# A Mamba scan on one core: where the next slot's gate product stands in TensorE's row

## The reference, cut to what matters

```python
xz = xn @ W_in                                  # 512 -> 2 x 1024
xs, res = jnp.split(xz, 2, axis=-1)
xs = silu(causal_conv(xs) + conv_b)
xdbc = xs @ W_xp                                # dt_r (128), B (16), C (16)
delta = softplus(dt_r @ W_dt + b_dt)
h_t = h_{t-1} * exp(delta * A) + delta * B * xs  # for 16 states n of each channel
y = sum_n(h_t * C) + xs * D
y = y * silu(res)                               # the gate
out = y @ W_out + x
```

## Time and profile before

| | |
|---|---|
| median of 3 runs | 1585.88 us (1583.93 to 1586.73) |
| the profiled execution, device time | 1580.36 us |
| its span, first to last instruction | 1578.3 us |
| mean granted TensorE clock | 0.972 of full |
| busy: PE, DVE, ACT, POOL | 1434.1, 1314.4, 744.0, 1077.5 us |
| slots (L1566 of slot 0 to the last sum of slot 31) | 61.7 to 995.9 us |
| shared experts and router after it | about 996 to 1208 us |

### The profile page before, as it was taken

How to read it: one execution, slowest core, us unless ns; L and a number is a source line. 1 busy time by engine, 2 the same in 40 slices (tenths; PEclk the granted TensorE clock), 3 DMA queues, 4 the chain that set the end, 5 groups by cost and what they waited for, 6 DMA issues and landing times.

```text
span 1578.3 us, 14721 instructions
## 1 busy us (share of the span) xinstructions
PE 1434.1 (91%) x4412; PEld 722.2 (46%) x4413; DVE 1314.4 (83%) x1931; ACT 744.0 (47%) x1160; POOL 1077.5 (68%) x545
## 2 busy tenths in 40 slices
PE   6678999899999799999888787999999999999997
PEld 3223444344344344444333333544445666667775
DVE  5589999999999999999999999464656868777772
ACT  4656666767656776655666665342000221211111
POOL 0299998999987999998999989150001446455453
PEclk9889999999999899999999999999999999999999
DMA  4540112510112510102410002231403788888995
GB/s 134 226 179 9 44 31 90 214 42 31 36 32 89 213 42 29 37 22 74 180 35 30 9 20 107 67 114 34 187 32 114 209 229 228 252 234 250 265 245 67
DMA packets 63822, 176.85 MB, mean 112 GB/s; under 512 B 10304, under 2 KB 15168, under 8 KB 55040
## 3 DMA queue, kind: packets, MB, share of 16 engines
q1 hardware_dynamic: 48128, 138.59, 25.4%
q0 software_dynamic: 15616, 37.32, 11.4%
HBM read 142.98 MB, written 32.85 MB: 111 GB/s over the span
## 4 chain that ended last, share of the span: by engine, by line
PE 42%; POOL 25%; DVE 19%; DMA 7%; issue 7%; ACT 1%; POOLq 0%; SPq 0%; DVEq 0%; ACTq 0%
POOL h L1368 14%; DVE h L957 10%; PE bank L1920 8%; PE bank L1569 8%; PE bank L1530 7%; DMA out<-y,slot_token 6%; DVE h L947 4%; POOL h L1355 4%; PE bank L1962 4%; PE bank L1537 4%; PE bank L1466 3%; POOL h L1373 3%; PE bank L1498 2%; PE bank L1488 2%; DVE xs L926 2%
## 5 line engine op out<-in xcount | busy, mean ns | idle before, releaser
L1368 POOL TENSOR_TENSOR h<-h,c_rep 128x2048 f32<-128x2048 f32 x128 | 578.6, 4526 | 20.0 <-DVE h L957 14.8
L1569 PE MATMUL bank<-h,ident 128*128 128x512 f32 x916 | 442.7, 627 | 73.5 <-POOL h L1368 57.8
L728 ACT ACTIVATE bank<-delta,a_neg 128x512 f32<-128x512 f32 x512 | 338.6, 684 | 151.7 <-DVE h L957 150.0
L1569 PEld LDWEIGHTS bank<-h,ident 128*128 128x128 f32 x916 | 181.9, 202 | 312.7 <-issue 219.3
L957 DVE TENSOR_TENSOR_SCAN h<-bank,state,h 128x512 f32<-128x512 f32 x256 | 306.9, 1265 | 1.3
L957 DVE TENSOR_TENSOR_SCAN h<-bank,h 128x512 f32<-128x512 f32 x256 | 291.5, 1204 | 3.7 <-ACT bank L728 2.7
L173 DVE STREAM_TRANSPOSE xT<-xg 32x256 f32<-32x256 f32 (+1 forms) x592 | 247.0, 417 | 24.6 <-DMA xg<-flat,slot_token 16.9
L947 DVE TENSOR_TENSOR h<-bank,b_rep 128x2048 f32<-128x2048 f32 (+1 forms) x105 | 228.8, 2179 | 21.6 <-ACT bank L719 18.3
L1920 PE MATMUL bank<-xT,w_ring 128*128 128x256 f32 x1024 | 227.4, 380 | 0.0
L1920 PEld LDWEIGHTS bank<-xT,w_ring 128*128 128x128 f32 x1024 | 193.8, 190 | 41.2 <-issue 16.6
L1729 POOL DMA_INDIRECT out<-y,slot_token x64 | 101.5, 1586 | 108.4 <-DMA out<-y,slot_token 63.6
(11 more groups left out here) (236 smaller groups left out, 1477.0 us busy)
## 6 DMA issues: line engine op xcount, KB each, us to landing
w_ring<-in_w SPq DMA_DIRECT2D x32, 1024.0 KB
b_rep<-bcd SPq DMA_DIRECT2D x16, 1024.0 KB, 4.8
c_rep<-bcd SPq DMA_DIRECT2D x16, 1024.0 KB, 5.0
w_ring<-in_w SPq DMA_DIRECT2D x32, 512.0 KB
w_in<-in_w_in_x SPq DMA_DIRECT2D x32, 256.0 KB, 2.6
w_res<-in_w_in_res SPq DMA_DIRECT2D x32, 256.0 KB, 2.6
xa<-in_x SPq DMA_DIRECT2D x20, 256.0 KB, 3.1
xb<-in_x SPq DMA_DIRECT2D x16, 256.0 KB, 2.7
```

What stands on the lines that cost most here:

```text
L728: eng.activation(da[j][:], delta[:, g % 2], ACT.Exp, scale=a_neg[:, col:col + 1])\
L1368: ins = eng.tensor_tensor(h[:, q], h[:, q], c_rep[:, Q * q:Q * q + Q, :], ALU.mult)
L1569: ins = eng.matmul(y_ps[:], c.ident[:], h[:, q, j, :], start=False, stop=(q == NQ - 1 and j == Q - 1))
```

## The change

In `gap_items`, z of the next slot goes into gap 1, behind what stands there, instead of gap 2. It stays in gap 2 where the slot g itself is leaving or dense. So 13 of 31 z products move: those made in slots 0, 1, 2, 6, 7, in 14 and 15, in 22 and 23, and in 27, 28, 29 and 30. Besides, in slot 31 the half projection `out` of segment 3 goes from gap 1 to gap 0.

```diff
             if g == LAST - 1:
                 gaps[3].append(("out", NSEG - 1, 0, 0))
             if g == LAST:
-                gaps[1].append(("out", NSEG - 1, 1, 0))
-            gaps[2].append(("z", (g + 1) // DC, g + 1, 0))
+                gaps[0].append(("out", NSEG - 1, 1, 0))
+            gaps[2 if leaving(g) or dense(g) else 1].append(("z", (g + 1) // DC, g + 1, 0))
             gaps[3].insert(0, ("dt", (g + 2) // DC, g + 2, 0))
```

## The result

| | before | after |
|---|---|---|
| median on the same chip | 1585.34 us (1581.91 to 1586.73, 8 runs) | 1577.24 us (1570.03 to 1579.27, 8 runs) |
| ratio | | 0.9939, 95% interval 0.9918 to 0.9960 |
| profiled execution, its span | 1580.36, 1578.3 us | 1579.27, 1577.5 us |
| mean granted TensorE clock | 0.972 | 0.971 |
| first L1566 to the first flat transpose (L1507), "the slots" | 934.2 us | 923.4 us |

The forecast was 1576.9. Two things stand apart from it, though: the slots gained 10.8 us and not 9.0, and in this execution 6.4 of them were lost again in a stretch for which nothing was expected. The eight times of after suggest that this is not always so: three lie at 1570.03 to 1571.54 and five at 1577.13 to 1579.27, with nothing between.

The account below looks back on a forecast made before the run. No engine bounds the whole (chain 42% TensorE, 25% GpSimd, 19% VectorE); GpSimd's 20.2 us of waits can shrink. 4.0 + 3.0 + 2.0 = 9.0 us, from median 1585.88 to 1576.9; gain 5.8 to 11.0, range 1573.0 to 1583.5.

Parts of the forecast that it names:

- Part A: Slots 0 to 2: z moved into TensorE's idle time takes away GpSimd's waits; 4.0 us, at the low clock 1.8.
- The first rival: Slot 2 at the low clock: slots 0 to 2 give only 1.8 us, sum 6.8, 1579.1 us; chance 0.24.
- the working: TensorE's slot 2 timed at full clock: quarter 1 from 139.7, then transposes and z, done at 147.2; GpSimd without wait.
- Part B: Slots 6, 7, 14, 15, 22, 23: z fills idle time ahead of slot 22's quarter 2; 3.0 us, all from slot 22.
- nothing lies in 6, 7, 14, 15 and 23: Moved z in these slots counts nothing: VectorE's busy row hides later sums; behind slot 23 GpSimd spreads nothing.
- Part C: Slots 27 to 31: VectorE's 1.33 us wait goes and the half projection fills idle time; 2.0 us, between 1.5 and 3.9.
- the upper bound of 3.9: Most that slots 27 to 31 could gain; the end at full clock was put at 992.1, against 995.9 now.
- the 1.8 us for a slow opening of slot 31: Price taken for slow d_diag and 16 slow instructions behind about 4 us of TensorE idle time; end 993.9, not 992.1.
- The 1.5 us put on the half projection: Slot 31: lower bound for slots 27 to 31, the moved projection alone, filling 1.48 us of idle time; 1.5 us.
- only slot 31 pays: By the skill's rule each of 13 slots would open slowly; the prediction claimed only slot 31 does.
- Whatever is gained by 996 is passed on whole.: Behind slot 31: TensorE is busy 209.0 of 212 us with shared experts, routed experts follow, so no gain is lost.
- a sign that it is wrong: Prediction is wrong if slots 3 to 7 lose part A's gain or time behind 996 doesn't shift by the same amount.

Follow-up runs that it names:

- the other kernel: The changed kernel with the four int32 casts (L1049) made by GpSimd behind its iotas instead of by VectorE; 1575.89 us median, ratio 0.9919.

## Why the prediction was right, and where it wasn't

**Part A, 4.0 us.** Measured 3.1 in the profiled pair (197.0 to 193.9 us for slots 0 to 5). The first rival, a slow quarter 1 in slot 2, is refuted: 0.16 us idle, 3.70 us, z done at 150.9, where the working gives 147.2 + 3.2 = 150.4 with this execution's later start. GpSimd's half spread at 155.57 waited for nothing. TensorE's stretch ended in slot 3 as worked out, but the sum came 3.4 us sooner and not 4.0, and VectorE still waited 1.77 us (2.10 before) ahead of the convolution at 179.98. Its scans of slot 4 start at 182.47, counted from slot 0's opening 3.1 us sooner, where the forecast had 4.0. One piece was wrong: slot 0's wait shrank from 1.26 to 0.60 us only, since quarter 1 took 6.59 us there behind 6.31 of idle time (5.21 behind 5.95 before), which made the moved z late. And what the sum treated as terms of single slots is one thing that needs all three.

**Part B, 3.0 us.** Measured 3.8 (54.9 to 51.1). The wait of 2.97 us in slot 23 went as forecast. Of the 3.8, 0.5 was only moved: slots 14 to 21 lasted 234.0 instead of 233.5. And part of the 3.8 is the slow sum in slot 22: against executions in which that sum was fast, the part is worth 2.1 us (53.2 to 51.1). That nothing lies in 6, 7, 14, 15 and 23 held.

**Part C, 2.0 us.** Measured 3.8 (126.9 to 123.1), nearly the upper bound of 3.9. VectorE's wait of 1.33 us for delta xs is gone, as forecast. The term mis-sized was the 1.8 us for a slow opening of slot 31 behind about 4 us of idle time. The slow opening came in slot 30 (2.08 us for d_diag, 8.98 for the sixteen instructions), while VectorE was busy without a pause; TensorE's row had no gap behind it, so ahead of slot 31 there were only 1.65 us, and no slow opening. The 1.5 us put on the half projection as the lower bound are right for it alone (1.3), but nothing is left of them beside z, which gives all 3.8.

**The price that the Trainium skill's rule names.** The prediction cited the rule against gathering idle time ("TensorE: Matmul & The Clock Gate", section "HAM oscillation — how this bites in real kernels"). It gathers, and the prediction was wrong that only slot 31 pays. Of the 13 slots that follow a moved z, slots 2, 8, 24, 28, 29 and 30 open more slowly than before (d_diag 1.86 to 2.08 us, 1.12 to 1.46 before, behind 3.02 to 5.40 us of idle time), 7, 15 and 16 as slowly as before, and 1, 3, 23 and 31 at full clock. In slots 28 to 30 this costs nothing: each lasts 26.2 us, VectorE's row has no gap there, and slots 27 to 29 took the same 26.2 before. What the runs add is the reverse: the holes that the old order had ahead of quarters 1 and 2 were on the path, and filling them took away slow sums that cost up to 3.0 us each (6.74 for 3.70).

**"Whatever is gained by 996 is passed on whole."** This step failed in the profiled execution, and the prediction had named it as a sign that it is wrong: 10.8 us were gained and 4.4 passed on (of which the later start of slot 0 hid 3.2 in this execution's span). TensorE's 209.0 busy of 212 us showed that it had no slack in that execution; I read it as a property of the stretch. VectorE's instruction order behind it, with the shared experts' multiplication behind the router, hangs on whether GpSimd's run holds VectorE. The before had the same exposure. Its profiled execution had the short cast, so no row pointed to it: of nine profiled executions with the cast on VectorE and GpSimd's run undivided, four had it short (75.0 us) and five long (81.4 to 83.0).

**The total.** 3.1 + 3.8 + 3.8 is 10.7 of the slots' 10.8; the 0.1 between lies in slots 6 to 21. The median moved by 8.1 and the forecast was 9.0. That this is closer than its terms is luck: two were too low by 2.6 together, one too high by 0.9, and a loss of 6.4 us, by the two groups in five of eight runs and in an unknown share of the runs of before, stood in no term. Side by side without that loss the change gives 11.6 us, above the forecast's range of 5.8 to 11.0.

## What to carry to other kernels

A product moved into idle time ahead of a sum pays twice, for the wait of whoever needs the sum and for the slow clock behind the hole; look for all the holes of a chain of slots, since filling one by itself may only shift it to the next. When times fall into two groups, compare an execution of each, stretch by stretch, before any of the difference is put down to a change. And a run of SBUF multiplications on GpSimd should not lie beside a chain of VectorE's that TensorE waits for, if GpSimd has a hole earlier.

## What the runs showed of the hardware

**VectorE held through several instructions of GpSimd.** The Trainium skill says in "SBUF — State Buffer", section "Who interferes with whom", that copies and casts on VectorE, in the modes that take two ports, and operations of two SBUF inputs contend with GpSimd for one pair of ports, and that the one which issues first blocks the other for its whole instruction. That a cast and a `tensor_tensor` of two SBUF inputs were held, while the `tensor_tensor` that reads PSUM just ahead of the cast took its usual 0.69 us, agrees. But one multiplication on GpSimd takes 1.23 us here (9.87 for eight), and the cast was held for 9.28 us, in the other kernel the `tensor_tensor` for 8.87, each time until the run of eight was over. In other executions of the same program, with the same 0.7 us between the start of GpSimd's second eight and the cast, VectorE came in at the end of the multiplication then running (0.68 us, against 0.22 with GpSimd idle), and GpSimd's eight took 10.34 instead of 9.87. What chooses between the two was not found; the only runs that varied it took the overlap away.

**The clock behind a hole isn't certain.** The same eight instructions behind 2.7 us of idle time took 3.70 us in two executions and 5.40 in four, and behind 3.4 us anything from 3.70 to 6.75; behind 1.84 us they took 5.40 in three. The order that leaves such holes also has times that spread: 1576.31 to 1587.31 us for z as before with GpSimd's run divided, 1569.01 to 1571.70 with z moved. That the clock makes all of that spread isn't shown; the profiled slots of the old order lie only 3.7 us apart.
